# Normalised rows split into 16-bit halves where they lie and transposed by DMA, in place of transposes on the matmul engine

## What is computed

```python
y = xp[:, :, 0, :]
for i in range(STAGES):
    conv = jnp.fft.irfft(jnp.fft.rfft(y, axis=1) * F[None, :, i, :], n=L, axis=1)
    y = conv * xp[:, :, i + 1, :]
...
x = _layernorm(x + _L0_attn_ref(x, ...), axis=-1)
x = _layernorm(x + _L0_ffn_ref(x, ...), axis=-1)
```

## Time and profile before

| | |
|---|---|
| median of 3 runs | 809.74 us (809.26 to 810.64) |
| the profiled execution | 810.85 us |
| its span, first to last instruction | 808.9 us |
| PE busy | 765.6 us (95%) |
| PE weight loads busy | 573.3 us (71%) |
| DVE busy | 556.9 us (69%) |
| ACT busy | 490.7 us (61%) |
| POOL busy | 434.4 us (54%) |
| mean granted clock of PE | 0.985 of full speed |
| PE's transposes (line 418), 128 instructions | 273 ns median each; eight in a stream take 0.87 us |
| the chain that ended last, by engine | PE 84%, DVE 6%, issue 3%, POOL 3% |

### The profile page before, as it was taken

The page is one execution under the profiler, slowest core; times in us unless marked ns, Lnnn a source line. Parts: engine busy times, 40 slices in busy tenths (PEclk is TensorE's granted clock), DMA queues, the critical chain, the costliest instruction groups (busy, mean ns, idle before and its releaser), DMA issues.

```text
span 808.9 us, 16504 instructions
## 1 busy us (share of the span) xinstructions
PE 765.6 (95%) x6068; PEld 573.3 (71%) x6068; DVE 556.9 (69%) x1173; ACT 490.7 (61%) x977; POOL 434.4 (54%) x564
## 2 busy tenths in 40 slices
PE   5999989999799999999999999789999999999993
PEld 4888868888588888888888877546655665566652
DVE  4777777777688888888887887645665565656551
ACT  3455554444377777777776664366577756776652
POOL 3445535445144444444444445687778778777452
PEclk9999999999899999999999999899999999999997
DMA  8659757998998888888889894311111221111001
GB/s 276 206 188 314 258 185 264 327 311 288 279 252 251 248 248 243 237 238 251 249 245 282 249 287 161 92 53 48 57 53 53 79 78 53 53 59 47 27 27 53
DMA packets 161151, 144.99 MB, mean 179 GB/s; under 512 B 4016, under 2 KB 144304, under 8 KB 160816
## 3 DMA queue, kind: packets, MB, share of 16 engines
q1 hardware_dynamic: 159232, 138.49, 56.6%
q10 hardware_dynamic: 1840, 5.44, 2.0%
HBM read 109.58 MB, written 34.34 MB: 178 GB/s over the span
## 4 chain that ended last, share of the span: by engine, by line
PE 84%; DVE 6%; issue 3%; POOL 3%; DMA 2%; ACT 1%; SPq 0%; DVEq 0%; ACTq 0%; POOLq 0%
PE bank L356 21%; PE bank L426 19%; PE bank L408 17%; PE bank L447 11%; PE bank L369 6%; DVE prod L745 3%; PE bank L390 3%; PE bank L392 2%; PE bank L391 2%; DVE yl L776 2%; PE bank L418 2%; POOL x L227 1%; DMA toep<-filter_rows 1%; DMA toep<-in_WP 1%; PE bank L468 1%
## 5 line engine op out<-in xcount | busy, mean ns | idle before, releaser
L908 POOL TENSOR_TENSOR y<-y,gate 128x256 f32<-128x256 f32 x192 | 139.2, 728 | 183.2 <-DVE y L768 171.2
L408 PE MATMUL bank<-prod,ei 128*128 128x256 f32 x720 | 201.4, 403 | 0.0
L356 PE MATMUL bank<-wps,xs 128*128 128x512 f32 x768 | 183.2, 398 | 10.6 <-DVE wps L703 8.3
L356 PEld LDWEIGHTS bank<-wps,xs 128*128 128x128 f32 x768 | 145.2, 191 | 42.6 <-issue 8.3
L935 POOL TENSOR_TENSOR xs<-xt,xs 128x256 fp32r<-128x256 f32 x128 | 93.2, 743 | 107.0 <-ACT xs L539 106.9
L426 PE MATMUL bank<-xh,wq 128*128 128x512 f16 x384 | 145.6, 379 | 2.7 <-DVE hf L808 1.5
L426 PE MATMUL bank<-xl,wq 128*128 128x512 f16 x384 | 145.5, 379 | 0.0
L927 POOL TENSOR_TENSOR hl<-hf,hh 128x512 f16<-128x512 f32 x96 | 110.2, 1157 | 53.6 <-ACT hh L596 53.5
L408 PEld LDWEIGHTS bank<-prod,ei 128*128 128x128 f32 x720 | 125.0, 193 | 10.5
L768 DVE SCALAR_TENSOR_TENSOR y<-bank,iscl,y 128x256 f32<-128x256 f32 x180 | 87.1, 484 | 64.4 <-PE bank L408 63.3
L808 DVE SCALAR_TENSOR_TENSOR hf<-bank,sg 128x512 f32<-128x512 f32 x96 | 64.2, 684 | 92.3 <-ACT sg L592 47.4
(11 more groups left out here) (65 smaller groups left out, 1247.7 us busy)
## 6 DMA issues: line engine op xcount, KB each, us to landing
toep<-filter_rows SPq DMA_DIRECT2D x43, 1024.0 KB, 7.5
gates<-toep SPq DMA_DIRECT2D x48, 512.0 KB, 4.0
gate<-gates SPq DMA_DIRECT2D x48, 512.0 KB, 4.3
xt<-in_XT SPq DMA_DIRECT2D x32, 512.0 KB, 5.2
xr<-in_X SPq DMA_DIRECT2D x16, 512.0 KB, 4.9
out_x<-oo SPq DMA_DIRECT2D x16, 512.0 KB, 3.3
toep<-filter_rows SPq DMA_DIRECT2D x10, 512.0 KB, 6.6
ei<-in_EI ACTq DMA_DIRECT2D x2, 1024.0 KB, 6.4
```

Of the source, the lines that this page charges most:

```text
L356: mm = pe.matmul(b_proj[n % PBK][:, :], xs[:, n % XSS, hx, k, :], wps[:, hw, k, p * 512:(p + 1) * 512], start=(k == 0 and q == 0), stop=(k ...
L408: mm = pe.matmul(b_out[n % 2][:, 0:W], ei[:, h, e0 * P:(e0 + 1) * P], prod[:, n % 3, h, :], start=(h == 0), stop=(h == 1))
L908: nc.gpsimd.tensor_tensor(y[:, u % NG, a, :], y[:, u % NG, a, :], gate[:, a, :], ALU.mult).then_inc(gated, 1)
```

## The change

PE's transposes, their PSUM banks and the identity matrix with its load are gone. ACT now rounds x1n to 16 bits where it lies (xhn, one activation of 1024 columns), and DVE writes the rest (xln, one operation of 1024 columns). SyncE's queue gets `turn(k)`: it waits for each half and issues one DMA of 256 KB that transposes it into xh or xl, and `ffn_up` waits for both DMAs. xh and xl have another order inside (sequence, feature half, position).

`split_x(k+2)` now stands at the end of ACT's block k, ahead of norm2(k-1); `low_x(k+1)` stays in DVE's block k; in the hand-over, split_x(1) follows norm1(1) and low_x(1) stands in step 15. `turn(k+2)` stands in the SyncE loop ahead of store(k) and behind load_rows(k+5) and a wait for the last up group of block k. For blocks 0 and 1 the turns stand in the short loop before it, each behind a wait for x1 and a row load. POOL has a wait for x1n before root(0, 2). PE's wait for `toep_out` has moved from step 11 to step 14.

```diff
--- before.py
+++ after.py
...
@@ -91,14 +91,15 @@
         xt = sb("xt", [P, XTS, KT, NB, P])
 
         with ExitStack() as ffn:
-            ident = sb("ident", [P, P], F32, ffn)
             wi = sb("wi", [P, 2, HID], I32, ffn)
             xr = sb("xr", [P, 2, NB, D], F32, ffn)
             wq = sb("wq", [P, 3, 2 * HID], F16, ffn)
-            xh = sb("xh", [P, 2, KT, NTOK], F16, ffn)
-            xl = sb("xl", [P, 2, KT, NTOK], F16, ffn)
+            xh = sb("xh", [P, 2, NB, KT, P], F16, ffn)
+            xl = sb("xl", [P, 2, NB, KT, P], F16, ffn)
             x1 = sb("x1", [P, 2, NB, D], F32, ffn)
             x1n = sb("x1n", [P, 3, NB, D], F32, ffn)
+            xhn = sb("xhn", [P, 2, NB, D], F16, ffn)
+            xln = sb("xln", [P, 2, NB, D], F16, ffn)
         xs = sb("xs", [P, XSS, 2, KT, P], F32R)
         bp = sb("bp", [P, (NS + 1) * D])
         posr = sb("posr", [P, 2, 2, P])
...
@@ -324,6 +324,12 @@
                                 sp.wait_ge(gated, u * NA + 4 * j + 4)
                             load_gate(u + 1, j)
 
+                def turn(k):
+                    for src, dst, ready, done in ((xhn, xh, xh_ready, xh_in), (xln, xl, xl_ready, xl_in)):
+                        sp.wait_ge(ready, k + 1)
+                        sp.dma_start_transpose(dst[:, k % 2].rearrange("p b t n -> p (b t) n"),
+                                               src[:, k % 2].rearrange("p b c -> p (b c)")).then_inc(done[k % 2], 16)
+
                 def store(k):
                     sp.wait_ge(oo_ready, k * NB + NB + 1)
                     sp.dma_start(oview[:, k], oo[:, k % 2]).then_inc(out_done[k % 2], 16)
@@ -332,12 +338,20 @@
                     sp.wait_ge(w_cast, e - 1)
                     load_weights(e)
                 for k in range(3):
-                    sp.wait_ge(x1_ready, k + 1)
-                    load_rows(k + 2)
+                    if k < 2:
+                        sp.wait_ge(x1_ready, k + 1)
+                        load_rows(k + 2)
+                        turn(k)
+                    else:
+                        sp.wait_ge(x1_ready, k + 1)
+                        load_rows(k + 2)
                 for k in range(NA):
                     if k + 5 < NA:
                         sp.wait_ge(x1_ready, k + 4)
                         load_rows(k + 5)
+                    if k + 2 < NA:
+                        sp.wait_ge(u_done, (k + 1) * HM)
+                        turn(k + 2)
                     store(k)
                 sp.wait_ge(out_done[0], NA // 2 * 16)
                 sp.wait_ge(out_done[1], NA // 2 * 16)
@@ -409,21 +423,12 @@
                                        start=(h == 0), stop=(h == 1))
                     mm.then_inc(r_done, 1)
 
-                def transposes(k):
-                    pe.wait_ge(x1n_ready, k * NB + NB)
-                    if k >= 1:
-                        pe.wait_ge(xl_ready, k * KT)
-                    for t in range(KT):
-                        for b in range(NB):
-                            mm = pe.transpose(b_t[t][:, b * P:(b + 1) * P], x1n[:, k % 3, b, t * P:(t + 1) * P], ident[:])
-                        mm.then_inc(tr_done, 1)
-
                 def ffn_up(k, m, wt, dst):
-                    pe.wait_ge(xh_ready, k * KT + KT)
-                    pe.wait_ge(xl_ready, k * KT + KT)
+                    pe.wait_ge(xh_in[k % 2], (k // 2 + 1) * 16)
+                    pe.wait_ge(xl_in[k % 2], (k // 2 + 1) * 16)
                     for t in range(KT):
                         for v in (xh, xl):
-                            mm = pe.matmul(dst[:, :], wt[:, t, m * P:(m + 1) * P], v[:, k % 2, t, :],
+                            mm = pe.matmul(dst[:, :], wt[:, t, m * P:(m + 1) * P], v[:, k % 2, :, t, :],
                                            start=(t == 0 and v is xh), stop=(t == KT - 1 and v is xl))
                     return mm
 
@@ -496,13 +501,10 @@
                         if k == 1 and u + 2 < NU:
                             pe.wait_ge(norm_sum, u + 2)
                             norm(u + 2)
-                        if k == 11 and u == NU - 1:
-                            pe.wait_ge(id_in, 16)
-                            pe.wait_ge(toep_out, NU * NQ)
-                            transposes(0)
                         if k == 14 and u == NU - 1:
                             pe.wait_ge(w_cast, 6)
                             pe.wait_ge(norm_sum, NU)
+                            pe.wait_ge(toep_out, NU * NQ)
                             gate_part(0, 0)
                         if k >= 2 and u < NU:
                             readout(u, k - 1)
@@ -519,8 +521,6 @@
                             gate_part(k, m)
                             up_part(k, m)
                         if m == 1:
-                            if k + 1 < NA:
-                                transposes(k + 1)
                             if k >= 1:
                                 if k == 1:
                                     pe.wait_ge(z_done, NU * NE)
@@ -581,9 +581,10 @@
                         w_cast, 1)
 
                 def split_x(k):
-                    act.wait_ge(tr_done, k * KT + KT)
-                    for t in range(KT):
-                        nc.scalar.activation(xh[:, k % 2, t, :], b_t[t][:, :], ACT.Copy, scale=XS).then_inc(xh_ready, 1)
+                    act.wait_ge(x1n_ready, k * NB + NB)
+                    if k >= 2:
+                        act.wait_ge(xh_in[k % 2], k // 2 * 16)
+                    nc.scalar.activation(xhn[:, k % 2], x1n[:, k % 3], ACT.Copy, scale=XS).then_inc(xh_ready, 1)
 
                 def silu(k, m):
                     act.wait_ge(g_done, k * HM + m + 1)
@@ -676,12 +677,11 @@
                                 split_x(0)
                             if k == 13:
                                 norm1(1, range(NB))
+                                split_x(1)
                 for k in range(NA):
                     silu(k, 0)
                     silu(k, 1)
                     high_h(k, 0)
-                    if k + 1 < NA:
-                        split_x(k + 1)
                     high_h(k, 1)
                     silu(k, 2)
                     if k + 2 < NA and k >= 1:
@@ -692,6 +692,8 @@
                         if m < HM - 1 and k + 2 < NA:
                             norm1(k + 2, range(2 * m - 6, 2 * m - 4))
                     high_h(k, HM - 1)
+                    if k + 2 < NA:
+                        split_x(k + 2)
                     if k >= 1:
                         norm2(k - 1)
                 norm2(NA - 1)
@@ -794,11 +796,11 @@
                     row_stats(x1[:, k % 2], 0, count)
 
                 def low_x(k):
-                    for t in range(KT):
-                        dve.wait_ge(xh_ready, k * KT + t + 1)
-                        nc.vector.scalar_tensor_tensor(out=xl[:, k % 2, t, :], in0=b_t[t][:, :], scalar=XS,
-                                                       in1=xh[:, k % 2, t, :], op0=ALU.mult,
-                                                       op1=ALU.subtract).then_inc(xl_ready, 1)
+                    dve.wait_ge(xh_ready, k + 1)
+                    if k >= 2:
+                        dve.wait_ge(xl_in[k % 2], k // 2 * 16)
+                    nc.vector.scalar_tensor_tensor(out=xln[:, k % 2], in0=x1n[:, k % 3], scalar=XS, in1=xhn[:, k % 2],
+                                                   op0=ALU.mult, op1=ALU.subtract).then_inc(xl_ready, 1)
 
                 def product(k, m):
                     dve.wait_ge(u_done, k * HM + m + 1)
@@ -878,10 +880,12 @@
                                 stats1((k - 6) // 3, (k - 6) // 3 + 1)
                             if k == 13:
                                 low_x(0)
+                            if k == NA - 1:
+                                low_x(1)
                 for k in range(NA):
                     product(k, 0)
                     product(k, 1)
-                    if k + 1 < NA:
+                    if 1 <= k < NA - 1:
                         low_x(k + 1)
                     if k + 2 < NA:
                         stats1(k + 2, count1(k))
@@ -946,6 +950,8 @@
                             pool.wait_ge(gated, u * NA + (k - 4) // 3 + 1)
                             add((k - 4) // 3)
                         if u == NU - 1 and k in (8, 11):
+                            if k >= 11:
+                                pool.wait_ge(x1n_ready, NB)
                             root(0, (k - 8) // 3 + 1)
                 pool.wait_ge(x1n_ready, NB)
                 add(2)
...
```

More of the change, by code:

```diff
@@ L41, with program @@
 QS = 1.0 / 127.0
-def program(nc, XT, X, WP, BP, WF, BFC, BFR, POSR, CM, CB, EF, EI, ONES, IDENT, WGT, WUT, WDT, OUT):
+def program(nc, XT, X, WP, BP, WF, BFC, BFR, POSR, CM, CB, EF, EI, ONES, WGT, WUT, WDT, OUT):
     fscr_ap = nc.dram_tensor("filter_rows", [NS * D, NL * 2], F16).ap()
@@ L131, in program @@
         b_proj = bank[2:6]
```

(9 more changed lines are left out.)

## The result

The changed kernel takes 812.92 us (median of 20 runs, 810.84 to 814.71), the kernel before 809.89 in the same comparison. The ratio is 1.0036, 95% interval 1.0028 to 1.0044: slower by 2.9 us. The profiled execution has a span of 811.9 us against 808.9.

A forecast was written before the change was run, and what follows sets the result against it. PE was taken to set the loop's pace, with POOL's last hl 0.45 us behind. Loop -4.2 and hand-over +4.4 gave +0.2 on the profiled 810.85, 811.05; less 1.11 to the median, 809.9 us, range 806.2 to 818.

The forecast's parts named there:

- hidden in the loop, late in the hand-over, low clock: Main case: DMA transposes cost nothing in the loop but delay block 0; 809.9 us, own range 807.8 to 812.5, chance 0.53.
- Part 1, the wait for hl: Loop: without PE's transposes, down starts 0.10 after hl, not 0.45; at most 0.35 us in each of 13 intervals.
- Part 2, the moved splits: Loop, ACT and DVE: moved splits change the gain by 0 to -1.6 us; 4.2 us gained, bounds 3.0 and 4.6.
- Part 3, landing: Hand-over: a DMA transpose lands 3.7 us after issue, bounds 3.0 and 5.0, at about 20 ns per 256-byte packet.
- Part 3, lateness: Hand-over: the first gate group waits for xl, 2.1 us late, bounds 1.4 and 3.5, reaching down(0) whole.
- Part 3, low clock: Hand-over: PE's idle stretch before the first gate group brings half clock, costing 2.3 us, bounds 0 and 2.7.
- Part 4: Loop: DMA transposes stay hidden with 2.5 us of cover, free while one moves in under 2.5 us.
- 1: Hand-over: no low clock or a quick transpose landing in 3.0 us; 806.9 us, chance 0.22.
- 2: Loop: slower transposes, over 2.5 us each, decide it through SP's queue order; 831 us, chance 0.17.
- 3: Loop: the 128x128 blocks of each transpose go one after another; near 1077 us, chance 0.05.
- 4: Loop: the whole removed PE time, 13 x 0.87 = 11.3 us, is gained without hand-over loss; 798.4 us, chance 0.03.

The follow-up runs named there:

- norm2_late: Changed kernel with last readouts before block 0's gate groups, POOL's last two hl pieces before the second root, norm2 behind the next block's high_h 1: 795.66 us.
- low_x_in_gap: Changed kernel with DVE's low half of block k+1 moved ahead of block k's first product, behind a wait for block k-1's last hl: 812.38 us.
- before_norm2_late: Kernel before with last readouts before block 0's gate groups, POOL's last two hl pieces before the second root, norm2 behind next block's high_h 1: 806.98 us.
- block0_on_pe: Changed kernel with block 0 transposed by PE at step 11 as before, blocks 1 to 15 by DMA: 808.97 us.
- filler: Changed kernel with 18 unread matmuls of 512 columns on PE ahead of the first gate group: 810.79 us.
- no_low_x: Changed kernel with DVE's low half cut to 8 columns and the DMA for xl turning the high half a second time: 811.26 us.

## Why the prediction was right or wrong

The forecast was no change, 809.9 us, for the case "hidden in the loop, late in the hand-over, low clock". That is the case that came. The measured 812.92 lies in the range, 3 us above the point and 0.4 above that case's own range (807.8 to 812.5). The loss of 0.36% is small but clear of the noise of 20 runs, so "no change" is not quite what came.

- **Part 1, the wait for hl.** Right in mechanism: down starts 0.10 after the last hl, with PE idle 0.55 before it (forecast 0.4 to 0.5). norm2_late shows it: with the wait gone, nine of 13 intervals are shorter by the whole 0.87. The size was half: 2.2 us gained where 4.2 was forecast. The step that failed is the margin of 0.45 us between the last hl and down. It took down's start from the chain (644.86), which counts from the end of the transposes, and hl's end from the timeline. In the timeline of the result section down starts at 644.70, so in the kernel before it stands 0.29 and not 0.45 behind hl. What a block can gain is then 0.29 - 0.10 = 0.19 and not 0.35; measured are 16.47 - 16.31 = 0.17.
- **Part 2, the moved splits.** ACT's 1.04 and DVE's 1.22 against 1.0 and 1.1 taken. That POOL's pair of hl would take 3.12 beside DVE's low half wasn't in the working. It cost next to nothing here: without it the interval is 16.28.
- **Part 3, landing.** xl landed 3.09 us after its issue, forecast 3.7, bounds 3.0 to 5.0; 24 ns a packet, forecast 20.
- **Part 3, lateness.** Counted from the add of chunk 0, the gate group is at 23.2 and was at 19.9: 3.3 late, forecast 2.1. The low half should have started 1.2 earlier than before and started 0.25 later (18.70 against 18.45), because the low clock behind PE's two idle stretches (3.19 us to 509.43, 3.82 us to 517.19) lay on the readouts at 518 to 522. low_x_in_gap has the same orders as the changed kernel until the last hl of block 0. In its profile the clock was 1.00 from 516 to 522, the low half started 17.20 after the add of chunk 0, 1.25 earlier than before as forecast, the gate group was 1.8 late, and down(0) stood at 45.04, not 47.37. So the mis-sized term is the missing 1.45, and its size depends on where the low clock falls. Both places are seen in profiles of either kind of kernel (early in the kernel before and norm2_late, late in before_norm2_late and block0_on_pe), so the change need not have moved it. How often each comes in the 20 runs isn't known; by the ratio the hand-over lost about 2.9 + 2.2 = 5.1 us, an estimate, and not 5.8.
- **Part 3, low clock.** From the gate group to down(0) 24.2 in place of 21.7, 2.5 us; forecast 2.3. filler, where that clock held, gave back 2.3 (ratios) and 2.5 (down(0)), and in no_low_x, where it held too, the stretch is 21.70. Here I count the cause as shown.
- **Part 4.** Right: no wait for a DMA in blocks 1 to 15. The cover of 2.5 us was real: in norm2_late the store goes out 3 us later, the block is 0.7 shorter, and PE does wait for xl in some blocks.
- **Rivals.** Of 1 the quick landing came (3.09), but not its other half: the clock fell. 2 and 3 (transposes decide the loop) fell: PE waits for no DMA after block 0, and a transpose moves in 1.5 us. 4 (intervals of 15.6) came true only after two exchanges in the loop, and then in nine of 13 intervals.

In sum: -0.6 by chance ahead of the change, +5.8 (with 1.45 of it from where the low clock fell in this execution), -2.2.

## What to carry to other kernels

Work taken off the engine that bounds is worth no more than the distance to the next wait, so look up when the last operand of the following step is ready, with both times from the timeline: here 0.29 of 0.87 us was free, and 0.17 was gained. Before giving a longer-latency path to the first block of a loop, move ahead of its wait everything in the in-order queue that doesn't need it: that alone turned a loss of 0.36% into a gain of 0.56%, of which 0.19% is there without the change too. Test a removal again after the cap is gone: the same change was then worth 1.4%.

## What the runs showed of the hardware

- POOL's subtraction on SBUF slows down while DVE makes the low half from two SBUF inputs: the pair of hl takes 3.12 in place of 2.27 us beside a low half of 1.22 (no_low_x, low_x_in_gap). Not every DVE operation on SBUF does this: beside the row statistics, which read one SBUF tile and write SBUF, an hl stays at 1.16 (at 647.85 in the kernel before), as it does beside operations with a PSUM operand.
- A DMA transpose of 256 KB between SBUF tiles lands 3.0 us after its issue at best, median 4.2 for xl behind other transfers, and moves in 1.5 us, an estimate from the packets of the changed kernel.
- 48 down matmuls take 5.40 us from first start to last end, behind a hole of PE or in a full stream. In a full stream they start 0.16 us before the modelled end of what stands before them (644.70 and 644.86 in the kernel before); behind a hole that is lost.
- Behind idle stretches of PE the low clock did not always come at the same place. In the changed kernel, with gaps of 3.19 and 3.82 us that end at 509.43 and 517.19, it was 1.00 from 510 to 516 and low from 518. In the kernel before, with a gap of 3.17 that ends at 510.03, it was low (0.50) from 510. Two profiles with the same orders in the hand-over (the changed kernel and low_x_in_gap) differ in this too, and by 2.3 us in down(0).
